# Three of an expert's five gate and up pairs as seven block products instead of eight, with the sums kept in PSUM

## What is computed

```python
def _mlp(h, wg, wu, wd):
    return jax.nn.silu(h @ wg) * (h @ wu) @ wd
# x: 4096 tokens x 512; F = 704, E = 16, K = 2, C = 640
vals, idx = jax.lax.top_k(softmax(x_tokens @ router_w + router_b), K)
expert_inputs = zeros((E, C, d)).at[idx_flat, pos_c].add(x_pair)
expert_outputs = jax.vmap(_mlp)(expert_inputs, w_gate, w_up, w_down)
gathered = expert_outputs[idx_flat, pos_c] * (vals_flat * within)[:, None]
return x + _mlp(x, sw_gate, sw_up, sw_down) + gathered.reshape(N, K, d).sum(axis=1)
```

## Time and profile before

| | us |
|---|---|
| median of three runs | 1819.67 |
| lowest, highest | 1819.43, 1821.1 |
| span of the profiled execution | 1818.3 |
| PE busy | 1804.8 (99%) |
| PEld (weight loads, beside PE) | 1598.7 (88%) |
| DVE busy | 873.3 (48%) |
| ACT busy | 800.0 (44%) |
| POOL busy | 922.2 (51%) |
| PE in the chain that ended last | 94% |

### The profile page before, as it was taken

One profiled execution on the slowest core, in us unless ns is written; L12 is line 12 of the kernel. 1 busy time (PEld: TensorE's weight loads), 2 busy tenths in 40 slices (PEclk: granted clock), 3 DMA queues, 4 the chain that ended last, 5 costly groups with the idle time before them and its releaser, 6 DMA issues.

```text
span 1818.3 us, 27202 instructions
## 1 busy us (share of the span) xinstructions
PE 1804.8 (99%) x9977; PEld 1598.7 (88%) x9977; DVE 873.3 (48%) x2067; ACT 800.0 (44%) x1574; POOL 922.2 (51%) x809
## 2 busy tenths in 40 slices
PE   9999999999999999999999999999999999999997
PEld 6888888888887878888999999999999999999997
DVE  6668777787745444332444324343334423443242
ACT  4555556555544343332444434444344434444331
POOL 3454464546653232225665656556665566656632
PEclk9999999999999999999999999999999999999999
DMA  8454555453552333225676676666666766667722
GB/s 319 147 134 122 151 140 150 134 143 95 147 116 40 47 52 68 37 42 103 161 141 132 163 156 134 135 150 158 147 140 126 164 149 140 145 138 163 145 41 29
DMA packets 254436, 229.35 MB, mean 126 GB/s; under 512 B 171712, under 2 KB 171968, under 8 KB 253024
## 3 DMA queue, kind: packets, MB, share of 16 engines
q1 hardware_dynamic: 228864, 174.51, 36.7%
q0 software_dynamic: 25440, 53.11, 17.3%
HBM read 138.80 MB, written 49.97 MB: 104 GB/s over the span
## 4 chain that ended last, share of the span: by engine, by line
PE 94%; DVE 2%; DMA 1%; issue 1%; POOL 1%; ACT 1%; SPq 0%; POOLq 0%; DVEq 0%; ACTq 0%
PE ps L72 66%; PE ps L1692 23%; PE ps L1002 3%; PE ps L1146 1%; PE ps L1008 0%; DMA buffer<-means 0%; ACT buffer L528 0%; DMA buffer<-in_x 0%; POOL buffer L481 0%; DMA means<-mean 0%; DVE buffer L832 0%; DVE stats L736 0%; DMA tokens_normed<-buffer 0%; ACT buffer L1491 0%; DMA buffer<-buffer 0%
## 5 line engine op out<-in xcount | busy, mean ns | idle before, releaser
L72 PE MATMUL ps<-buffer,buffer 128*128 128x320 f32 (+1 forms) x6900 | 1239.1, 341 | 1.3 <-DVE buffer L832 0.8
L72 PEld LDWEIGHTS ps<-buffer,buffer 128*128 128x128 f32 x6900 | 1121.0, 188 | 107.5 <-issue 1.5
L1426 POOL TENSOR_TENSOR buffer<-buffer,buffer 128x512 fp32r<-128x512 f32 x289 | 380.4, 1480 | 251.6 <-ACT buffer L1491 251.1
L1692 PE MATMUL ps<-buffer,buffer 128*128 128x512 f32 (+1 forms) x1921 | 437.6, 388 | 0.4 <-DVE buffer L1624 0.4
L1692 PEld LDWEIGHTS ps<-buffer,buffer 128*128 128x128 f32 x1921 | 356.9, 188 | 73.9 <-issue 1.2
L1533 ACT ACTIVATE buffer<-ps 128x320 f32<-128x320 f32 (+1 forms) x240 | 112.5, 469 | 599.6 <-PE ps L72 594.0
L1491 ACT ACTIVATE buffer<-buffer 128x512 fp32r<-128x512 f32 (+1 forms) x491 | 293.4, 652 | 163.4 <-PE ps L1692 90.6
L1599 DVE TENSOR_TENSOR ps<-ps,buffer 128x320 f32<-128x320 f32 (+2 forms) x198 | 100.2, 506 | 487.5 <-ACT buffer L1533 477.0
L1480 POOL DMA_INDIRECT out_tokens<-buffer,slot_list x79 | 124.0, 1569 | 185.5 <-DVE buffer L1636 177.3
L520 POOL DMA_INDIRECT slots<-pairs,slot_u x64 | 63.6, 994 | 181.8 <-DVE slot_u L989 164.8
L528 ACT ACTIVATE buffer<-buffer 128x512 fp32r<-128x512 f32 (+1 forms) x212 | 127.0, 683 | 19.9 <-DMA buffer<-buffer 15.2
(11 more groups left out here) (134 smaller groups left out, 1094.0 us busy)
## 6 DMA issues: line engine op xcount, KB each, us to landing
buffer<-in_wts SPq DMA_DIRECT2D x289, 256.0 KB
buffer<-in_xT SPq DMA_DIRECT2D x8, 1024.0 KB, 5.5
buffer<-in_ctxT SPq DMA_DIRECT2D x8, 1024.0 KB, 8.2
out_tokens<-buffer SPq DMA_DIRECT2D x8, 1024.0 KB, 4.3
tokens_normed<-buffer SPq DMA_DIRECT2D x32, 256.0 KB, 3.1
out_tokens<-buffer POOLq DMA_DIRECT2D x32, 256.0 KB, 5.1
buffer<-in_x SPq DMA_DIRECT2D x7, 1024.0 KB, 5.5
buffer<-combiners_top SPq DMA_DIRECT2D x6, 1024.0 KB, 4.9
```

The lines of the kernel that those rows point to most:

```text
L72: last = pe.matmul(out, left, right, start=(c == 0 and i == 0), stop=(c == len(parts) - 1 and i == 2))
L1426: pool.tensor_tensor(wl[n % RING][:], wraw[n % RAW][:], wh[n % RING][:].bitcast(F32), ALU.subtract).then_inc(s_wl, 1)
L1692: ins = pe.matmul(down_bank[(n + i) % 2][:, part_cols], left, right, start=(c == 0 and k == 0), stop=(c == FC - 1 and k == len(passes) - 1))
```

## The change

Pairs 0 and 1 (`PLAIN`) keep 24 matmuls a unit. For pairs 2, 3 and 4 (`CROSSED`) gate and up form a 2 x 2 block matrix with the two halves of the contraction, and the tokens a 2 x 2 block matrix of these with the two halves of 320 tokens; its product is made of seven block products instead of eight, each of 6 matmuls of 320 columns. DVE forms four sums of weight blocks per pair (`prepare`) and four of token blocks per expert (`token_sums`), each split in high and low parts (`prepare_sums`, `token_sum_hi`, `token_sum_lo`). PE accumulates several products in one PSUM bank; ACT copies four intermediate values of a bank to SBUF (`kept1`, `kept7`, `kept6`, `kept5`), and DVE adds them to the other banks in PSUM (`pair_combined`). Banks 6 and 7 now hold the first and last gate sums, so a unit's product goes to bank 2 or 3 (`product_bank`), the bank that a later unit's up sums use. POOL makes the low parts of a pair's chunks behind DVE's low part of its sums. The gathered tokens share rows with the scaled output, halves of the token words are now put together by ACT alone, and tokens are split in three parts instead of five. The weights leave the ring and have fixed places; the shared groups are computed as before.

The core of the diff, with some waits left out inside the functions:

```diff
-    xn = at(57, [ET, 2 * D], U16)
+    xn = at(89, [ET, 2 * D], U16)
...
+        prepared[g, 0] = [chunk(e, GU + i) for i in range(3)]
+        prepared[g, 1] = [chunk(e, GU + i) for i in range(3, FC)]
+        if e + 1 < E:
+            prepared[g, 2] = [chunk(e + 1, 0), chunk(e + 1, 1)]
+            prepared[g, 3] = [chunk(e + 1, 2), chunk(e + 1, 3)]
+            prepared[g, 4] = [chunk(e + 1, 4), chunk(e + 1, 5)]
+            prepared[g, "down0"] = [chunk(e + 1, 6), chunk(e + 1, 7)]
+            prepared[g, "down2"] = [chunk(e + 1, 8), chunk(e + 1, 9), chunk(e + 1, GU - 1)]
...
+            if i == 3 and job > 1:
+                turn_tokens(job - 1)
+            load_weights(n)
...
     def gpsimd(pool):
+                if g >= B and c == 0:
+                    if g + 1 < NG:
+                        gather(g + 1)
+                    pool.wait_ge(s_tl, len(TOKEN_PARTS) * (g - B + 1))
+                prepare(g, c)
...
     def scalar(act):
+        def pair_products(e, p):
+            act.wait_ge(s_prod, PER_PAIR * q + 1)
+            copy(kept1[:], chain[:, 0:HALF]).then_inc(s_keep, 1)
+            if p > PLAIN:
+                h_hi(e, p - 1, 0)
+            act.wait_ge(s_prod, PER_PAIR * q + 2)
+            copy(kept7[:], cross[:, 0:HALF]).then_inc(s_keep, 1)
+            h_hi(e, p - 1, 1)
+            act.wait_ge(s_prod, PER_PAIR * q + 3)
+            copy(kept6[:], chain[:, 0:HALF]).then_inc(s_keep, 1)
+            prepare(g, p)
+            act.wait_ge(s_prod, PER_PAIR * q + 5)
+            copy(kept5[:], chain[:, 0:HALF]).then_inc(s_keep, 1)
+            act.wait_ge(s_comb, 4 * q + 1)
+            act.activation(gates[0][:], first_bank[:, 0:HALF], ACT.Silu).then_inc(s_silu, 1)
+            prepare_sums(g, p)
+            act.wait_ge(s_comb, 4 * q + 4)
+            act.activation(gates[1][:], last_bank[:, 0:HALF], ACT.Silu).then_inc(s_silu, 1)
...
+            for p in range(PLAIN):
+                for j in range(2):
+                    act.wait_ge(s_unit, PER_EXPERT * e + 2 * p + j + 1)
+                    act.activation(gates[j][:], chain_bank[j][:, 0:HALF], ACT.Silu).then_inc(s_silu, 1)
+                    if (p, j) != (0, 0):
+                        h_hi(e, p - (j == 0), 1 - j)
+                prepare(g, p)
...
     def vector(dve):
+                    product(e, p, j, cross_bank[j][:, 0:HALF])
+                    if (p, j) != (0, 0):
+                        h_lo(e, p - (j == 0), 1 - j)
...
+        def pair_ended(e, p):
+            h_lo(e, p, 0)
+            product(e, p, 1, chain_bank[p % 2][:, 0:HALF])
+            h_lo(e, p, 1)
+        def pair_combined(e, p):
+            if p > PLAIN:
+                pair_ended(e, p - 1)
+            else:
+                h_lo(e, p - 1, 1)
+            dve.tensor_tensor(first, first, kept1[:], ALU.add).then_inc(s_comb, 1)
+            prepare(g, p)
+            dve.tensor_tensor(chain, chain, kept7[:], ALU.add).then_inc(s_comb, 1)
+            dve.tensor_tensor(cross, cross, kept6[:], ALU.add).then_inc(s_comb, 1)
+            product(e, p, 0, cross)
+            dve.tensor_tensor(last, last, kept5[:], ALU.add).then_inc(s_comb, 1)
+            prepare_sums(g, p)
...
+            prepare(g, "down0")
+            scaled(g, 0)
+            token_lo(e + 1, 0)
+            token_sums(e + 1, 0)
+            prepare_sums(g, "down0")
+            scaled(g, 1)
+            token_lo(e + 1, 1)
+            token_sums(e + 1, 1)
+            prepare(g, "down2")
+            scaled(g, 2)
+            token_lo(e + 1, 2)
+            token_sums(e + 1, 2)
+            prepare_sums(g, "down2")
+            scaled(g, 3)
+            scaled(g, 4)
...
     def tensor(pe):
+        def plain(e, p, j):
+            elif p > 0:
+                pe.wait_ge(s_hl, unit_no[(g, p - 1, j)] + 1)
...
+            for bank, i in ((chain_bank[j], 2 * p), (cross_bank[j], 2 * p + 1)):
...
+        def pair(e, p):
+            product(chain, *a11, *b11, True)
+            if p < PLAIN + 2:
+                pe.wait_ge(s_hl, unit_no[(g, PLAIN - 1, p - PLAIN)] + 1)
+            product(cross, *s3, *t3, True)
+            pe.wait_ge(s_keep, 4 * q + 1)
+            product(chain, *s2, *t2, False)
+            product(first_bank, *a12, *b21, True)
+            pe.wait_ge(s_keep, 4 * q + 3)
+            product(chain, *s1, *t1, False)
+            pe.wait_ge(s_keep, 4 * q + 2)
+            product(cross, *a22, *t4, False)
+            product(last_bank, *s4, *b22, True)
```

More of the change, by code:

```diff
@@ L57 @@
 BANKS = 8
-ROWS = 98
+ROWS = 99
 XS = 3
@@ L1341, in rows_of @@
         return P if c < FC - 1 else FH
[L1343 to L1356, removed]
@@ new lines, in scalar @@
+                if g == 0 and c == 4:
+                    split(WC - 1)
+                prepare(g, c)
+                prepare_sums(g, c)
+            h_hi_shared(u)
+            for t in range(NT):
+                if g == B - 1:
+                    words(0, t)
+                    if t == 1:
+                        token_hi(0, 0)
+                prepare(g, f"down{t}")
+                prepare_sums(g, f"down{t}")
+            if g == B - 1:
+                token_hi(0, 1)
+                words(0, ET - 1)
+                token_hi(0, 2)
+                for part in range(len(TOKEN_PARTS)):
+                    token_sum_hi(0, part)
@@ new lines, in vector @@
+                if c == FC - 1:
+                    h_lo_shared(u)
+                for name, b in router.get((g, c), []):
+                    step(name, b)
+                prepare(g, c)
+                prepare_sums(g, c)
+            for t in range(NT):
+                prepare(g, f"down{t}")
+                prepare_sums(g, f"down{t}")
+                scaled(g, t)
+                if g == B - 1 and t % 2 == 1:
+                    token_lo(0, t // 2)
+                    token_sums(0, t // 2)
+                if g == B - 1 and t == NT - 1:
+                    token_lo(0, 2)
+                    token_sums(0, 2)
@@ L1639, in tensor, with product @@
     def tensor(pe):
         step = attn["tensor"](pe)
+        def product(bank, hi, lo, x_hi, x_lo, first):
+            for c in range(2):
+                passes = [(hi[:, c], x_hi[:, c]), (hi[:, c], x_lo[:, c]), (lo[:, c], x_hi[:, c])]
+                for i, (left, right) in enumerate(passes):
+                    ins = pe.matmul(bank[:, 0:HALF], left, right, start=(first and c == 0 and i == 0),
+                                    stop=(c == 1 and i == 2), skip_group_check=not first)
+            ins.then_inc(s_prod, 1)
@@ new lines, in tensor @@
+        for e in range(E):
+            g = B + e
+            for p in range(PLAIN):
+                for j in range(2):
+                    plain(e, p, j)
+            for p in range(PLAIN, FC - 1):
+                pair(e, p)
+            mixed_hi, mixed_lo = single_hi[GU - 1], single_lo[GU - 1]
+            pe.wait_ge(s_wl, chunk(e, GU - 1) + 1)
+            for j, bank in enumerate((first_bank, last_bank)):
+                pe.wait_ge(s_silu, unit_no[(g, FC - 2, j)] + 1)
+                three_pass(pe, bank[:, 0:HALF], [
+                    (mixed_hi[:, d * P:(d + 1) * P], mixed_lo[:, d * P:(d + 1) * P], xh[:, j, d, :], xl[:, j, d, :])
+                    for d in range(NC)]).then_inc(s_unit, 1)
+            for t in range(ET):
+                down(g, t)
```

672 lines of the change are left out of this document (450 added, 222 removed).

## The result

The changed kernel takes 1890.26 us (median of four runs, 1888.41 to 1890.7), 1.038 times the kernel before (95% interval 1.0368 to 1.0398). The forecast was 1891.0. The profiled execution has a span of 1886.7 us, 68.4 more than the 1818.3 to which the earlier trace rows belong; it was the fastest of the four executions, 1.9 us under their median.

A forecast was written before the change was run, and what follows sets the result against it. PE, busy 99%, was taken to bound the kernel. From 1818.3 us, expert holes 91.7 and 18.2, entry 3.6, less 42.2 saved, gave 1889.6 of span, 1891.0 as median; range 1867 to 1914, chance 0.80.

The forecast's parts named there:

- pair 2: First crossed pair: PE waits for a low part at M2 and ACT's first kept copy at M3, 1.31 us an expert.
- pairs 3 and 4 together: Later crossed pairs: PE waits for ACT's kept copies at M3 and M5, 0.36 us each, 0.72 an expert.
- The saving: Crossed pairs of all 16 experts: 288 fewer matmuls of 320 columns at 0.1466 us, 42.2 us less.
- The plain units: Pairs 0 and 1: PE waits for DVE's low part queued behind the next half's SiLU, two holes of 1.85 us an expert.
- Down: Down phase before tile 4: PE waits for DVE's scaling of tile 2, 0.23 plus 0.7 us beside POOL, 0.93.
- no contention 0.23: Lower bound of the hole before down's tile 4, if DVE never waits beside POOL: 0.23 us.
- the port term: Down phase: DVE waiting beside POOL's subtractions of SBUF inputs, taken as 0.7 us more before tile 4.
- The entry: Last shared group before the first expert: token parts come late behind DVE's scaling of tile 3, 3.6 us net.
- Rival 1: Low parts come a half earlier, plain holes go and pair 2's shrinks to about 0.4: 1818 us, chance 0.05.
- Rival 2: Low parts come early, kept copies hide under M2 and M4, down has slack, only the entry is left: 1781 us, chance 0.02.
- Rival 3: PE's clock falls in the experts' holes, 1.4 to 3.2 us each: 1914 to 1942 us, chance 0.07.
- Rival 4: Gathers and transposes slip over 2.5 us, weights late, ACT and PE stand at pair 3: 1907 to 1925 us, chance 0.06.

The follow-up runs named there:

- the banks run: Changed kernel with the plain units' products put in banks 6 and 7, PE waiting for DVE's product instead of its low part: 1876.9 us.
- the run with all orders: Changed kernel with plain products in banks 6 and 7, later token transposes on SP, and ACT's and DVE's orders changed: 1827.6 us.

## Why the prediction was right, and where it was not

The times at which the matmuls start give each term. Per expert in us:

| step | predicted | measured |
|---|---|---|
| wait before unit (1,0) | 1.85 | 1.72 |
| wait before unit (1,1) | 1.85 | 1.72 |
| pair 2 | 1.31 | 1.25 |
| pairs 3 and 4 together | 0.72 | 0.61 |
| mixed unit to down's tile 0 | 0.28 | 0.16 |
| before down's tile 4 | 0.93 | 0.96 |
| sum | 6.94 | 6.42 (6.47 with small ones) |
| entry to the first expert, over before | 3.6 | 8.6 |

- **The saving.** 288 matmuls fewer are 42.2 us, and the spacing of those that stay is unchanged. 16 experts of holes are 102.3 us and the entry 8.6, less 0.3 that the kernel before had in its experts: 110.6 - 42.2 = 68.4, which is the difference of the spans.
- **The plain units.** Mechanism, place and rank right; each link of the chain was a little quicker (ACT's SiLU starts 0.20 and not 0.26 behind PE's issue when its wait is on the instruction itself, DVE behind ACT 0.03 to 0.04), which makes the 0.13. Two runs that undo it in different ways, and the one with the transposes moved, show it to be worth 55 us: in each, PE no longer waits there.
- **Pair 2.** Right in its parts as well: 0.90 at M2, 0.35 at M3. That ACT's three weight copies set it was argued, and is shown by the banks run, where M2 waits for nothing and M3's hole is 1.24.
- **Down.** The sum 0.23 + 0.7 hit, its split did not. DVE's instructions beside POOL last 1.04 us longer than alone; taking that off the 0.96, DVE's own queue would just reach the tile. That is worked out from durations; the only run in which POOL no longer stood there had no hole, but it was late everywhere else. The bound "no contention 0.23" was 0.3 too high, the port term 0.3 too low.
- **The entry** was the mis-sized term: 8.6 us for 3.6. The hole before the first expert was forecast at 4.2 and measured 4.4, but the step failed twice. I looked at tiles 1 to 3 only, and the weight sums of chunks 6 and 7 stand ahead of the low part that tile 0 needs: a hole of 2.3 us. And the 4.4 us hole was priced as idle alone; behind it the clock stands at half for 5 us, 19 matmuls, which is 2.3 us more. The windows of the changed kernel, clock third from the right:

```profile
882.00:887.00 5.00, 0.78 (x4) 0.38 (x3) 4.31 (x10) 1.04 (x2) 4.26 (x5) 0.79 0.81 139
887.00:889.00 2.00, 2.00 (x8) 2.00 (x9) 1.97 (x5) 0.79 (x2) 1.70 (x2) 0.50 0.88 227
```

- Two errors of 5 us (the entry, too low) and 8 us (the experts, too high) thus stand against each other. The span of the profiled execution was forecast at 1889.6 and came out at 1886.7; that the median missed by only 0.7 is luck. The method was good to about 8 us, not to 1.
- **Rival 1** gave 1818 for the plain holes gone. Undone by order it was 1869, by banks 1877, by banks with SP's order 1835. Its own price forgot the loop of the weights, and that pair 2's hole stays.
- **Rival 2**, the sums hidden, isn't what the changed kernel does, but 1799.0 against its 1781 shows that most of it can be had by banks and order alone. What is left is 22 us of holes and slow matmuls: 4 in the last shared group, 18 in three holes of 0.3 to 0.4 us in nearly every expert.
- **Rival 3**, the clock: not in the steady state, whose window shows 1.00, but at the entry, and in the runs with longer holes. Its price was summed wrongly: 1.4 to 3.2 us behind each of four holes in 16 experts are 90 to 205 us, and 1914 to 1942 counts one hole an expert.
- **Rival 4**, late weights, was closer than its chance of 0.06 says. The cover was taken as 2.5 us. In the changed kernel chunk 3 landed 0.3 to 1.8 us before ACT's copy of it, 1.0 in the middle, in all experts but the first. In the timeline of one expert the load is issued at 1099.69 behind the transposes, lands at 1102.63, and ACT's second copy of the pair starts at 1103.52:

```profile
1099.69 39.02 SPq L1457 DMA_DIRECT2D buffer<-in_wts  x14
...
1103.00 1.15 ACT L1583 ACTIVATE buffer<-buffer 128x512 fp32r<-128x512 f32 x2
```

It held, so the forecast did, but late weights were the next wait in each run that took the plain holes away.

## What to carry to other kernels

When results are kept in the bank that the next product uses, PE waits for the last reader and no longer for the first; walk the chain to that last reader through the order of each engine's queue, since a high part queued behind the next half's activation waits for that whole half. When a hole is closed, ask at once which load or buffer the faster engine will meet next: here 55 us of closed holes gave 13 us until SP's queue was reordered, and two more steps gave 7 of 43 us until POOL's was. Keep GpSimd's work with two SBUF inputs off the stretches where VectorE does the same, and if it can't be moved away, see whom it meets.

## What the runs showed of the hardware

- **Short holes leave the clock alone, longer ones do not always.** The changed kernel's holes of 1.7 us, two per expert, never lowered PE's granted clock from 1.00. Of thirteen holes of 1.8 to 2.7 us in the experts of the run with all orders, two (2.0 and 2.4) were followed by 12 or so matmuls at 0.267 us, and the longest, 2.7, was not: which of them lower it stays open. The same hole of 2.2 us in the last shared group's first down tile stands in ten of the runs, and was followed by half clock in seven of them, not in the changed kernel. All 18 holes of 3.0 to 5.1 us, over all runs, were followed by half clock, most of them by 3 to 6 us of matmuls at it; none of the 228 holes of 1.0 to 1.8 us from the shared groups on was. The Trainium skill ("TensorE: Matmul & The Clock Gate", A second HAM failure mode) has short idles between groups bring the clock down; for holes under 1.8 us no run here shows that.
- **A DVE instruction with two SBUF inputs can wait for a whole row of GpSimd's**, 4.62 us for 0.28 in the run where POOL is not held, where I had taken one.
- **PE behind a hole** needs 0.05 us to the weight load and 0.1 us more for the second matmul; so in all the holes that were looked at.
